# Gated cross-attention chain on one core: the opening stage merged into the first attention block

## What is computed

```python
q_big = einsum('bshk,hkq->bshq', (hidden_q @ Wq.T).reshape(B, S, H, K), w_kc_q)   # 192 wide
q_big = rope(q_big);  kv_r = rope(kv_c)            # kv_c: the context, 4 x 64 rows of 64
scores = (q_big @ W_qr) . (kv_r @ W_kr);  attn = softmax(scores)
ctx_lat = (attn @ kv_r) @ w_kc_kv.T;  out = ctx_lat @ Wo.T
```

## Time and profile before

| what | us |
|---|---|
| median of 3 runs | 1043.04 |
| lowest and highest run | 1038.9, 1043.93 |
| span of the profiled execution, first to last instruction | 1044.7 |
| TensorE matmul busy | 904.6 (87%) |
| VectorE busy | 570.6 (55%) |
| GpSimd busy | 418.6 (40%) |
| ScalarE busy | 344.9 (33%) |

### The profile page before, as it was taken

The page is one execution under the profiler, slowest core; times in us unless marked ns, Lnnn a source line. Parts: engine busy times, 40 slices in busy tenths (PEclk is TensorE's granted clock), DMA queues, the critical chain, the costliest instruction groups (busy, mean ns, idle before and its releaser), DMA issues. The chain is left out here.

```text
span 1044.7 us, 14430 instructions
## 1 busy us (share of the span) xinstructions
PE 904.6 (87%) x4607; PEld 697.1 (67%) x4607; DVE 570.6 (55%) x1078; ACT 344.9 (33%) x620; POOL 418.6 (40%) x328
## 2 busy tenths in 40 slices
PE   1999999598779999999948977799469798999996
PEld 1788788497646666666747976778358665565654
DVE  5567777555834434444377988678676632222321
ACT  2254444241013333344234434354234331221221
POOL 2477666303048888875432212360170005022222
PEclk9899999897879999999979998999569979999998
DMA  6511210004935543664822000000000094222210
GB/s 240 178 44 44 85 43 1 0 2 149 409 86 87 89 75 69 117 121 54 231 81 81 1 23 14 22 15 1 11 1 1 15 425 191 76 46 40 40 30 10
DMA packets 38432, 84.79 MB, mean 81 GB/s; under 512 B 9709, under 2 KB 27501, under 8 KB 35726
## 3 DMA queue, kind: packets, MB, share of 16 engines
q1 hardware_dynamic: 22190, 64.63, 17.6%
q0 software_dynamic: 16176, 19.31, 11.2%
HBM read 71.23 MB, written 20.68 MB: 88 GB/s over the span
## 5 line engine op out<-in xcount | busy, mean ns | idle before, releaser
L2481 PE MATMUL ffn_GU<-ffn_W,ffn_XTB 128*128 x252 | 91.2, 485 | 2.4 <-DVE ffn_XTB L2389 1.8
L1965 PE MATMUL ffn_GU<-ffn_W,ffn_XTB 128*128 x184 | 85.0, 605 | 0.0
L1786 POOL DMA_INDIRECT out_x<-ffn_YB,ffn_XB x23 | 35.8, 1558 | 117.9 <-DVE ffn_YB L1914 115.9
L2191 POOL DMA_INDIRECT kept_MARKED<-scratch_rows,kept_IDX x63 | 62.7, 994 | 50.8 <-DMA scratch_rows<-ffn_WEIGHT 31.8
L2373 DVE TENSOR_TENSOR ffn_GB<-ffn_GU,ffn_BIAS 128x352 f32<-128x352 f32 x63 | 33.1, 525 | 88.8 <-PE ffn_GU L2481 74.9
L2481 PEld LDWEIGHTS ffn_GU<-ffn_W,ffn_XTB 128*128 128x128 f32 x252 | 43.7, 191 | 35.2 <-issue 21.1
L2512 PE MATMUL ffn_DN<-ffn_W,ffn_HT 96*128 x252 | 64.9, 380 | 0.0
L1992 PE MATMUL ffn_DN<-ffn_W,ffn_HT 128*128 (+1 forms) x248 | 60.4, 388 | 3.5 <-issue 2.8
L2229 ACT ACTIVATE ffn_HG<-ffn_GB 128x176 f32<-128x176 f32 x63 | 22.2, 352 | 116.4 <-DVE ffn_GB L2373 74.6
L1903 DVE COPY ffn_XTB<-ffn_XP 128x256 f32<-128x256 f32 x23 | 9.8, 425 | 86.9 <-PE ffn_XP L1974 86.9
L1965 PEld LDWEIGHTS ffn_GU<-ffn_W,ffn_XTB 128*128 128x128 f32 x184 | 33.1, 189 | 36.0 <-issue 33.5
(11 more groups left out here) (500 smaller groups left out, 2485.7 us busy)
## 6 DMA issues: line engine op xcount, KB each, us to landing
ffn_W<-in_f_w SPq DMA_DIRECT2D x9, 1536.0 KB, 6.6
ffn_W<-in_f_w SPq DMA_DIRECT2D x16, 608.0 KB, 18.2
attn_W<-in_L_pairs SPq DMA_DIRECT2D x8, 1088.0 KB, 4.9
scratch_rows<-in_rows_empty SPq DMA_DIRECT2D x1, 2967.0 KB, 14.1
ffn_XB<-scratch_rows SPq DMA_DIRECT2D x23, 129.0 KB, 2.1
ffn_BIAS<-in_f_bias SPq DMA_DIRECT2D x1, 2816.0 KB, 15.0
kept_STAGE<-in_f_w SPq DMA_DIRECT2D x1, 2048.0 KB, 8.5
kept_STAGE<-in_L_pairs SPq DMA_DIRECT2D x2, 768.0 KB, 6.7
```

The source lines that it names most:

```text
L1786: pool.indirect_dma_start(out[:, :], bass.IndirectOffsetOnAxis(ap=XB[:, i % NB, D:D + 1].bitcast(I32), axis=0), YB[:, i % 3, :], None, bou ...
L1965: last = pe.matmul(GU[:, m, :], x, weights(e, k * 2 * HID3 + m * HID3, HID3), start=k == 0, stop=k == KD - 1)
L2191: pool.indirect_dma_start(XB[:, i % NB, :], None, DR["rows0"][:, :], bass.IndirectOffsetOnAxis(ap=IDX[:, i:i + 1], axis=0)).then_inc(rows_ ...
L2481: last = pe.matmul(GU[:, n % 2, 0:2 * HID], XTB[:, i % 2, k * P:(k + 1) * P], flat[:, bass.ds(e * WIDTH0 + k * 2 * HID, 2 * HID)], start=k ...
```

## The change

The opening block is gone. Its work stands inside the block of the first attention, in this order:
- **SP**: section 0 of pair 0's W, x in two halves, the rest of W, COS, SIN, the four context arrays, then (after a wait for pair 0's last low part) W of pair 1, and only then the four scratch fills. The loop begins at pair 2.
- **ScalarE**: issues the DMAs of gates and identity on its own queue, takes the tanh, splits section 0, takes the roots of half 0, splits sections 1 and 2, then query_weights(0), the high parts of half 0's two banks, the roots of half 1, the high parts of half 1's two banks, step 0.
- **GpSimd**: constants and mask, with the mask's cast (VectorE's before), the three low parts of W, the cast of the identity, then the rotation of the context with its copies into KVB.
- **VectorE**: clears KVB, measures tiles 0 to 5, normalises half 0, query_weights(0), low parts of half 0, measures tiles 6 and 7, normalises half 1, low parts of half 1, step 0.
- **TensorE**: query_weights(0), transposes of half 0, query(0, 0), key_value_weights(0), transposes of half 1, query(0, 1). query(0, 0) and query(0, 1) wait for two low parts each, keys(0, 0) waits for KVB. Half 1 is turned in the two score banks (`ST`), half 0 in `QB` banks 0 and 1.

```diff
@@ the opening block, removed whole @@
...
-@block.sync
-def _(sp):
-    for dst, src in ((graw, "gates"), (IDENT, "ident"), (kvt, "kvT"), (kvs, "kvT_swapped"), (kcos, "kcos"), (ksin, "ksin")):
-        sp.dma_start(dst[:, :], A[src]).then_inc(loaded, 16)
-    sp.dma_start(X[:, :, :], A["x"].rearrange("(t p) d -> p t d", p=P)).then_inc(x_loaded, 16)
-    sp.wait_ge(x_loaded, 16)
-
-@block.scalar
-def _(act):
-    act.wait_ge(loaded, 96)
-    act.activation(GATE[:, :], graw[:, :], ACT.Tanh).then_inc(gates_done, 1)
-
...
-    for part in KVB:
-        rope.inc(dve.memset(part[:, :, :].bitcast(F32), 0.0))
-    dve.wait_ge(loaded, 96)
-    rope.inc(dve.tensor_copy(IDENTB[:, :], IDENT[:, :]))
-    rope.inc(dve.tensor_tensor(prod[:, 0, :], kvt[:, :], kcos[:, :], ALU.mult))
-    rope.inc(dve.tensor_tensor(prod[:, 1, :], kvs[:, :], ksin[:, :], ALU.mult))
-    rope.wait(dve)
...
-    dve.wait_ge(x_loaded, 16)
-    for t in range(T):
-        measure(dve, x_stats, t)
@@ latent_rope @@
-nrm = norm(ctx, "a0", [QB[:, j, :] for j in range(4)])
...
+XBANK = (QB[:, 0, :], QB[:, 1, :], ST[:, 0, :], ST[:, 1, :])
...
@@ sync @@
-        sp.dma_start(W[:, :], A["L0_pairs"][0]).then_inc(w_in, 16)
+        sp.dma_start(W[:, 0:O_KR], A["L0_pairs"][0, :, 0:O_KR]).then_inc(w_first, 16)
+        for h in range(2):
+            tiles = slice(T // 2 * h, T // 2 * (h + 1))
+            sp.dma_start(X[:, tiles, :], A["x"].rearrange("(t p) d -> p t d", p=P)[:, tiles, :]).then_inc(x_in[h], 16)
+        sp.dma_start(W[:, O_KR:PAIR_END], A["L0_pairs"][0, :, O_KR:PAIR_END]).then_inc(w_in, 16)
         sp.dma_start(COS[:, :, :], A["qcos"]).then_inc(tables, 16)
         sp.dma_start(SIN[:, :, :], A["qsin"]).then_inc(tables, 16)
+        for dst, src in ((kvt, "kvT"), (kvs, "kvT_swapped"), (kcos, "kcos"), (ksin, "ksin")):
+            sp.dma_start(dst[:, :], A[src]).then_inc(kv_in, 16)
+        sp.wait_ge(w_lo[2], 1)
+        sp.dma_start(W[:, :], A["L0_pairs"][1]).then_inc(w_in, 16)
         sp.dma_start(DR["rows3"][:, :], A["rows_empty"]).then_inc(scratch_set, 16)
         sp.dma_start(DR["sum_a"][:, :], A["zeros"]).then_inc(scratch_set, 16)
         sp.dma_start(DR["sum_b"][:, :], A["zeros"]).then_inc(scratch_set, 16)
         sp.dma_start(DR["rows0"][B * S:B * S + 1, :], A["zero_row"]).then_inc(scratch_set, 16)
-        with sp.Fori(1, NP) as p:
+        with sp.Fori(2, NP) as p:
             sp.wait_ge(w_lo[2], p)
             sp.dma_start(W[:, :], A["L0_pairs"][bass.ds(p, 1), :, :].rearrange("a p n -> (a p) n")).then_inc(w_in, 16)
@@ gpsimd @@
+        pool.memset(EPS[:, :], 1e-5).then_inc(consts_set, 1)
+        pool.memset(ONES[:, :], 1.0)
+        pool.memset(maskf[:, :], 0.0).then_inc(mask_steps, 1)
+        pool.wait_ge(mask_steps, 1)
+        pool.affine_select(out=maskf[:, :], in_=maskf[:, :], compare_op=ALU.is_ge, fill=MASKED, base=0, pattern=[[-1, L]], channel_multiplier=1).then_inc(mask_steps, 1)
+        pool.wait_ge(mask_steps, 2)
+        pool.tensor_copy(MASK[:, :], maskf[:, :])
         for c in range(3):
             low(0, c)
+        pool.wait_ge(ident_in, 16)
+        pool.tensor_copy(IDENTB[:, :], IDENT[:, :])
+
+        def turned_keys():
+            pool.wait_ge(kv_in, 64)
+            rope.inc(pool.tensor_tensor(prod[:, 0, :], kvt[:, :], kcos[:, :], ALU.mult))
+            rope.inc(pool.tensor_tensor(prod[:, 1, :], kvs[:, :], ksin[:, :], ALU.mult))
+            rope.wait(pool)
+            rope.inc(pool.tensor_tensor(kvt[:, :], prod[:, 0, :], prod[:, 1, :], ALU.add))
+            rope.wait(pool)
+            rope.inc(pool.tensor_copy(KV[0][:, :], kvt[:, :]))
+            rope.wait(pool)
+            rope.inc(pool.tensor_tensor(KV[1][:, :], kvt[:, :], KV[0][:, :].bitcast(F32), ALU.subtract))
+            rope.wait(pool)
+            pool.wait_ge(kvb_cleared, 2)
+            for n in range(4):
+                i, h = divmod(n, 2)
+                rows = slice(64 * h, 64 * h + 64)
+                pool.tensor_copy(KVB[i][rows, :, L * h:L * h + L], KV[i][rows, :].bitcast(F32).rearrange("p (b l) -> p b l", b=B)).then_inc(kvb_ready, 1)
+                pool.wait_ge(kvb_ready, n + 1)
+        turned_keys()
@@ scalar @@
+            if first:
+                act.wait_ge(w_first if c == 0 else w_in, 16)
+            elif c == 0:
                 act.wait_ge(w_in, 16 * (p + 1))
-                if not first:
-                    act.wait_ge(c_ps, 2 * p)
+                act.wait_ge(c_ps, 2 * p)
...
-        nrm["deviation"](act)
-        for c in range(3):
-            high(0, c, True)
-        nrm["scalar"](act)
+        act.dma_start(graw[:, :], A["gates"]).then_inc(gates_in, 16)
+        act.dma_start(IDENT[:, :], A["ident"]).then_inc(ident_in, 16)
+        act.wait_ge(gates_in, 16)
+        act.activation(GATE[:, :], graw[:, :], ACT.Tanh).then_inc(gates_done, 1)
+        high(0, 0, True)
+        act.wait_ge(consts_set, 1)
+        deviation(0)
+        high(0, 1, True)
+        high(0, 2, True)
         query_weights(0)
+        rows_high(0)
+        rows_high(1)
+        deviation(1)
+        rows_high(2)
+        rows_high(3)
@@ vector @@
-        nrm["vector"](dve)
-        nrm["vector_low"](dve)
...
+        def normalise_rows(h):
+            tiles = slice(T // 2 * h, T // 2 * (h + 1))
+            dve.wait_ge(std_ready, h + 1)
+            dve.reciprocal(RSTD[:, tiles], STD[:, tiles]).then_inc(inverted, 1)
+            dve.wait_ge(inverted, h + 1)
+            for t in range(T // 2 * h, T // 2 * (h + 1)):
+                dve.tensor_scalar(XN[:, t, :], X[:, t, :], MOM[:, t, 0:1], RSTD[:, t:t + 1],
+                                  ALU.subtract, ALU.mult).then_inc(xn_ready, 1)
+
+        def rows_low(j):
+            dve.wait_ge(xt_hi, j + 1)
+            dve.tensor_tensor(xt[1][:, j % 2, half(j)], XBANK[j], xt[0][:, j % 2, half(j)].bitcast(F32), ALU.subtract).then_inc(xt_ready, 1)
+
+        for part in KVB:
+            dve.memset(part[:, :, :].bitcast(F32), 0.0).then_inc(kvb_cleared, 1)
+        for t in range(T - 2):
+            if t % (T // 2) == 0:
+                dve.wait_ge(x_in[t // (T // 2)], 16)
+            measure(dve, x_stats, t).then_inc(measured, 1)
+        normalise_rows(0)
         query_weights(0)
+        rows_low(0)
+        rows_low(1)
+        for t in (T - 2, T - 1):
+            measure(dve, x_stats, t).then_inc(measured, 1)
+        normalise_rows(1)
+        rows_low(2)
+        rows_low(3)
@@ tensor @@
-        nrm["tensor"](pe)
-        pe.wait_ge(nrm["ready"], 4)
+        def turn_rows(j):
+            if j == 0:
+                pe.wait_ge(ident_in, 16)
+            pe.wait_ge(xn_ready, T // 2 * (j // 2 + 1))
+            for q in range(T // 2):
+                last = pe.transpose(XBANK[j][:, q * P:(q + 1) * P], XN[:, j // 2 * (T // 2) + q, (j % 2) * P:(j % 2 + 1) * P], IDENT[:, :])
+            last.then_inc(xt_turned, 1)
...
+            if first and g < 2:
+                pe.wait_ge(xt_ready, 2 * (g + 1))
...
+            if first and t == 0:
+                pe.wait_ge(kvb_ready, 4)
...
+        turn_rows(0)
+        turn_rows(1)
...
             key_value_weights(p, age)
-            query(p, 1)
-            keys(p, 0)
+            if age < 1:
+                turn_rows(2)
+                turn_rows(3)
+            query(p, 1, age < 1)
+            keys(p, 0, age < 1)
```

More of the change, by code:

```diff
@@ L309, in wide @@
                     return ap.rearrange("p (n l) -> p n l", l=L)
+                kvt = sbuf(ctx, "kvt", [P, B * L])
+                kvs = sbuf(ctx, "kvs", [P, B * L])
+                kcos = sbuf(ctx, "kcos", [P, B * L])
+                ksin = sbuf(ctx, "ksin", [P, B * L])
+                prod = sbuf(ctx, "prod", [P, 2, B * L])
+                graw = sbuf(ctx, "graw", [P, 8])
+                maskf = sbuf(ctx, "maskf", [P, L])
                 QB = psum(ctx, "QB", [P, 4, 512])
@@ L313, in latent_rope, with half @@
                 TURNED = TR[:, :, :].rearrange("p a n -> p (a n)")
-                nrm = norm(ctx, "a0", [QB[:, j, :] for j in range(4)])
-                tables = sem(ctx, "tables")
+                XBANK = (QB[:, 0, :], QB[:, 1, :], ST[:, 0, :], ST[:, 1, :])
+                tables, kv_in, gates_in, ident_in, w_first = (sem(ctx, s) for s in ("tables", "kv_in", "gates_in", "ident_in", "w_first"))
+                x_in = [sem(ctx, f"x_in_{h}") for h in range(2)]
+                consts_set, mask_steps, gates_done, kvb_cleared = (sem(ctx, s) for s in ("consts_set", "mask_steps", "gates_done", "kvb_cleared"))
+                rope, kvb_ready = Count(sem(ctx, "rope_steps")), sem(ctx, "kvb_ready")
+                x_stats, measured, std_ready, inverted, xn_ready = (sem(ctx, s) for s in ("x_stats", "x_measured", "x_std", "x_inverse", "x_normalised"))
+                xt_turned, xt_hi, xt_ready = (sem(ctx, s) for s in ("xt_turned", "xt_hi", "xt_ready"))
+                def half(j):
+                    return slice(j // 2 * HALF, j // 2 * HALF + HALF)
```

(28 more changed lines are left out.)

36 lines of the change are left out of this document (removed).

## The result

| | before | changed |
|---|---|---|
| median, 5 runs each | 1040.48 | 1033.15 |
| lowest to highest | 1038.9 to 1043.93 | 1031.29 to 1036.77 |
| ratio, 95% interval | | 0.9934 (0.991 to 0.9959) |
| span of the profiled execution | 1044.7 | 1030.6 |

The change gains 7.3 us by the medians; the ratio says 4.3 to 9.4. 11 were forecast (1032.0, from a median of before that two more runs have lowered by 2.6). The two spans differ by 14.1 us, and that is not the change: each run of the changed kernel lies 1.75 above its span, so that the profiled execution of before was, by the same step, a run of 1046.5, above all of the five.

What follows compares the result with a forecast made beforehand. TensorE was taken to set the pace once pairs run, so gains lie ahead of pair 0. 14.4 − 3.2 − 0.5 + 0.2 = 10.9, say 11 us, off the median 1043.04 gave 1032.0; range 1028.0 to 1037.5.

Steps and rivals of the forecast that it cites:

- the forecast itself: Whole kernel: 9 to 12.5 us gained, given a chance of 56%.
- A late start, 6 to 9 gained: Rival, opening of pair 0: x later, VectorE slowed, more waits, or low clock from the start; about 1035.5; 17%.
- VectorE slowed by 1.4: Part of the late-start rival (17%): normalising a half of x doubles from 1.4 us by contention with GpSimd.
- Loads: Opening DMAs: section 0 lands at 4.5, x halves at 6.2 and 7.5, rest of W at 9.3, context at 13.5.
- First half of x: Ahead of query(0, 0): half 0 normalised by 11.1, turned by 12.9; query(0, 0) at 14.3, 14.4 us earlier.
- Table load: ScalarE's load of 1.28 us for the square root: hidden, over before 8.4; otherwise the sum loses some 1.5.
- Second half: Half 1 of x, between query(0, 0) and query(0, 1): adds 1.8 and 1.4; query(0, 1) at 23.3, 11.2 left.
- readout: query(0, 0)'s readout on VectorE, behind half 1's low parts, at 23.3: keys(0, 0) waits 0.5, 10.7 left.
- rotation: Context rotation on GpSimd: ends by 20.2, or 21.9 at the late bound; keys(0, 0) needs it at 26.5; costs nothing.
- W of pair 1: Its load, ahead of the scratch fills: lands near 18 to 20; nothing either way, at worst one load's 5.0.
- The clock: TensorE in query(0, 0): slow pace kept, about 4.5 us; a better-clock rival had 2.8, 1030.4, at 15%.
- A low clock from the start: Part of the late-start rival (17%): each 8 transposes on TensorE take 3.7 instead of 1.8 us.

Runs made afterwards that it cites:

- the first experiment: Changed kernel, with GpSimd waiting for the normalised half 0 before its low parts of sections 1 and 2; ratio to before 0.9885 (0.9853 to 0.9917).

## Why the prediction was right, and which term was mis-sized
The range holds the result, but the forecast itself, 9 to 12.5 gained, does not: 7.3 by the medians and 7.7 to 8.0 by the positions lie in the rival "A late start, 6 to 9 gained" (17%), of which the part "VectorE slowed by 1.4" is what happened, at 2.5. That the median, 1033.15, came within 1.2 of 1032.0 is partly luck, since the median of before fell by 2.6.

- **Where the gain comes from.** Right: a later pair is TensorE's, and the earlier start is kept. ScalarE's table load, at 233.87 before for the roots at the attention's end, stands at 225.13 after: 8.7 of shift behind all eight pairs. What the last 0.7 over the 8.0 at pair 7 is was not tried.
- **Loads.** Right within 0.23 for section 0 and 0.05 for x. Section 0's split followed the tanh without a wait, so it had landed by 4.73 and perhaps earlier.
- **First half of x: the step that was off.** "normalises half 0 (0.2 + 1.4)". Normalising took 3.9: 2.5 of the 3.4 us missed. The text had the effect as an unshown 1.4 at most and took zero. It should not have bounded it by doubling: GpSimd's two instructions ran for 3.07 us, and at their end, 13.72, VectorE had ended only two of the four. The page "GPSIMD Engine Reference" of the Trainium skill (Specifications, its first table) names contention with GpSimd for VectorE's instructions "in a 2-port perf mode or with two SBUF inputs". The product of 1.29 in the run with the rotation back agrees with its second case; that the normalising form falls under the first, no run shows.
- **Table load: wrong on its place.** "the load does not stand behind the wait" was read from a place with one wait. This place has two. It cost the start 0.65, and by moving the work further under GpSimd's low parts it brought 1.6 of the 2.5 above, as the run with the wait moved shows. By the rule of the page "ScalarE: Activation LUTs" of the Trainium skill (Step-by-step: what each stage is for) the load stands right before its instruction; here that was so, at 1.28 and with the roots 1.29 behind the load's start, so the drain that the page adds was not seen.
- The remaining 0.25 is sums of small latencies. 2.5 + 0.65 + 0.25 = 3.4.
- **Second half, readout, rotation, W of pair 1.** Right in order and in what waits. query(0, 1) came 9.02 behind query(0, 0), 9.0 were said, but this agreement is luck: query(0, 0) stayed at the low pace for longer (5.2 to the next product, 4.5 before), and the turning of half 1 took 1.03 where 1.8 was said. keys(0, 0) began at 29.86, right behind VectorE's last low part (29.30 + 0.41). GpSimd's copies ended at 19.4 (20.2 said) with over 10 us to spare. The order of the scratch fills is worth nothing, as shown.
- **The clock.** Keeping query(0, 0) at its slow pace was right, but the evidence given was not. "16 transposes at 0.23 each under a granted 1.00" reads the view for more than it holds: here 8 transposes take 1.94 at first, as before, and 1.03 at 24.11. So TensorE began at its lower pace in both kernels. The traces have no record of the clock ahead of 22.09 (before) and 22.74 (changed), and the view prints 1.00 up to there. A low clock from the start was no rival; it was so before as well, and on both sides of the comparison. The rule of the page "TensorE: Matmul & The Clock Gate" of the Trainium skill (Part 1), that the lower level is the default, agrees with these rows.

## What to carry to other kernels
Before work is moved to GpSimd, look at what VectorE does in the same stretch with no operand in PSUM, and price an overlap as VectorE standing still until GpSimd's instruction ends, unless rows show that form running on (the statistics did). Splitting an operand in halves helps only if the second half is not put between the first half's use and the work that everything waits for: count to the mark behind both. Where a kernel opens with scattered TensorE work, filling its idle stretches with products that nobody reads can be a cheap gain: here 3.1 us at the mark.

## What the hardware showed that was not expected
- **Two of VectorE's forms stood still for GpSimd, two others did not.** Four normalising instructions took 1.38 alone and 3.90 beside two subtractions of GpSimd; the source view gives 400 to 1884 ns for one:
```profile
L557 DVE TENSOR_SCALAR XN<-X,MOM,RSTD x8: 400/410/1884, 10.3 to 20.3; 128x256 f32<-128x256 f32 x8
```
The product of two operands outside PSUM took 1.29 instead of 0.42 with the rotation back. GpSimd paid nothing here (3.07; alone 3.04, in the first experiment), but 3.24 where VectorE had started first, with the constants' wait moved. The statistics at 6.15 ran beside GpSimd's first low part at 0.43, and low parts with one operand in PSUM ran beside its rotation at 0.69, both at their usual length. Why these forms differ was not tried.
- **One wait or two decides where a table load goes.** Moving one wait of ScalarE moved the load from 8.46 to 5.61. The tanh, with one wait ahead of it, fits: its load ran at 1.68 in the changed kernel and the tanh at 4.61. That it is the number of waits and not the semaphore is inferred from these and the earlier trace rows alone.
- **Transposes were followed by a rise.** In the kernel before TensorE had only its 16 transposes behind it, 18.07 to 21.74, when its weight product started at 25.05. TensorE's timeline of that kernel shows its matmuls 0.11 apart, and from 25.6 on 0.21:
```profile
25.24 0.27 PE L96 MATMUL attn_QB<-attn_WS_lo,attn_WS_hi 128*128 128x192 f32 x1
...
25.35 0.28 PE L97 MATMUL attn_QB<-attn_WS_hi,attn_WS_lo 128*128 128x192 f32 x1
...
25.62 0.41 PE L96 MATMUL attn_QB<-attn_WS_lo,attn_WS_hi 128*128 128x192 f32 x1
...
25.83 0.41 PE L97 MATMUL attn_QB<-attn_WS_hi,attn_WS_lo 128*128 128x192 f32 x1
```
So the upper level was reached with transposes alone behind it, and lost again near 25.5, after 3.30 us without work and half a us of this product. The page "TensorE: Matmul & The Clock Gate" of the Trainium skill (Part 4) says that transposes do not count as such work; these rows speak against it.
- **Time scatters with the mean clock.** Of the changed kernel's five runs, the one at 1031.29 had a mean granted clock of 0.930 and the one at 1036.77 had 0.920, by the same program. What sets this from run to run stays open.
